# K's mixed input in halves, and written-out orders for the first two blocks' steps of an RWKV-like attention layer

## The reference

```python
xn = ln(x); sx = shift(xn) - xn
xxx = tanh((xn + sx * maa_x) @ maa_w1)            # five groups of 32 channels
x5 = xn + sx * (maa_stack + xxx @ maa_w2)         # five mixed inputs: K, W, V, R, G
w = exp(-exp(time_decay + tanh(x5.W @ decay_w1) @ decay_w2))
r, k, v = x5.R @ Wr.T, x5.K @ Wk.T, x5.V @ Wv.T;  g = silu(x5.G @ Wg.T)
for t in tokens:                                  # per head of 16 channels, s is 16 x 16
    a = k_t (outer) v_t
    out_t = r_t @ (faaaa * a + s);  s = a + w_t * s
att = groupnorm(out) * gn_w + gn_b
x = x + (att * g) @ Wo.T
xn2 = ln(x); sx2 = shift(xn2) - xn2
kk = relu((xn2 + sx2 * ffn_maa_k) @ ffn_Wk.T) ** 2
x = x + sigmoid((xn2 + sx2 * ffn_maa_r) @ ffn_Wr.T) * (kk @ ffn_Wv.T)
```

## Time and profile before

| | |
|---|---|
| median of three runs | 1561.68 us (1560.24 to 1562.09) |
| the profiled execution | 1565.06 us |
| its span, first to last instruction | 1563.2 us |
| TensorE (matmul) busy | 1509.9 us, 97% |
| VectorE, GpSimd, ScalarE busy | 909.0, 593.5, 516.0 us |
| step 0, step 1, a middle step (kt0 to kt0) | 72.00, 93.67, 93.04 us |

### The profile page before, as it was taken

The page is one execution under the profiler, slowest core; times in us unless marked ns, Lnnn a source line. Parts: engine busy times, 40 slices in busy tenths (PEclk is TensorE's granted clock), DMA queues, the critical chain, the costliest instruction groups (busy, mean ns, idle before and its releaser), DMA issues.

```text
span 1563.2 us, 50425 instructions
## 1 busy us (share of the span) xinstructions
PE 1509.9 (97%) x22156; PEld 1093.8 (70%) x22156; DVE 909.0 (58%) x1990; ACT 516.0 (33%) x910; POOL 593.5 (38%) x512
## 2 busy tenths in 40 slices
PE   8989999999999999999999999999999999999888
PEld 7867776768677676776767677676776767777564
DVE  3566666466584755667466575655667465564542
ACT  1323333324233233423324333233423333332332
POOL 3343524335261532625244261432625244262331
PEclk9999999999999999999999999999999999999899
DMA  7011102011020211102011010201102011020110
GB/s 292 25 27 48 40 5 67 25 37 52 11 70 15 61 31 34 55 4 74 17 39 52 26 54 14 66 26 35 55 5 74 17 39 53 13 61 7 47 38 27
DMA packets 56442, 68.01 MB, mean 44 GB/s; under 512 B 23264, under 2 KB 40032, under 8 KB 55200
## 3 DMA queue, kind: packets, MB, share of 16 engines
q1 hardware_dynamic: 56224, 64.79, 13.7%
HBM read 43.75 MB, written 8.39 MB: 33 GB/s over the span
## 4 chain that ended last, share of the span: by engine, by line
PE 81%; DVE 13%; POOL 3%; issue 2%; ACT 1%; DVEq 0%; ACTq 0%; POOLq 0%
PE pair L1163 30%; PE pair L1171 20%; PE at_ps L1092 4%; DVE x L718 3%; PE at_ps L1085 3%; PE pair L1179 3%; PE att_ps L1154 2%; PE pair L1252 2%; POOL x L488 2%; PE pair L1216 2%; PE pair L1254 2%; DVE cu L631 2%; PE pair L1195 2%; PE att_ps L1141 1%; PE pair L1259 1%
## 5 line engine op out<-in xcount | busy, mean ns | idle before, releaser
L1163 PE MATMUL pair<-x,wts 128*128 128x256 f32 x2016 | 459.4, 382 | 8.2 <-POOL x L488 8.1
L1163 PEld LDWEIGHTS pair<-x,wts 128*128 128x128 f32 x2016 | 374.2, 190 | 64.3 <-ACT zt L934 9.0
L488 POOL TENSOR_TENSOR x<-x,xnT 128x1024 f32<-128x1024 f32 x79 | 171.8, 2176 | 294.0 <-DVE x L718 294.0
L718 DVE SCALAR_TENSOR_TENSOR x<-pair,vecs,sx 128x256 f32<-128x256 f32 x316 | 130.5, 475 | 239.4 <-PE pair L1195 136.7
L915 ACT ACTIVATE at<-at_ps 128x512 f32<-128x512 f32 x128 | 76.0, 594 | 291.3 <-PE at_ps L1092 253.7
L1163 PE MATMUL pair<-yT,wts 128*128 128x256 f32 x512 | 119.1, 386 | 1.5 <-DVE yT L806 1.5
L1171 PE MATMUL pair<-wts,cen 128*128 128x512 f32 x240 | 112.9, 613 | 3.2 <-DVE x L718 2.5
L1092 PE MATMUL at_ps<-rm,kc 128*16 128x128 f32 (+1 forms) x2048 | 111.1, 276 | 3.2 <-issue 3.2
L1171 PE MATMUL pair<-wts,yT 128*128 128x512 f32 x240 | 110.9, 605 | 1.7 <-POOL yT L526 1.7
L1171 PE MATMUL pair<-wts,sx 128*128 128x512 f32 x240 | 109.1, 598 | 0.0
L1163 PEld LDWEIGHTS pair<-yT,wts 128*128 128x128 f32 x512 | 95.9, 192 | 16.8 <-DVE gT L750 2.9
(11 more groups left out here) (197 smaller groups left out, 2486.6 us busy)
## 6 DMA issues: line engine op xcount, KB each, us to landing
rm<-rst SPq DMA_DIRECT2D x1024, 12.0 KB, 1.8
xu<-in_x SPq DMA_DIRECT2D x16, 512.0 KB
wts<-in_wts SPq DMA_DIRECT2D x8, 1024.0 KB, 14.4
kvs<-in_s SPq DMA_DIRECT2D x32, 256.0 KB, 3.0
s<-in_s SPq DMA_DIRECT2D x32, 256.0 KB, 3.0
x<-in_x SPq DMA_DIRECT2D x15, 512.0 KB, 4.3
out<-sx SPq DMA_DIRECT2D x15, 512.0 KB, 2.9
prev<-in_prev SPq DMA_DIRECT2D x32, 4.0 KB, 3.9
```

The lines of the kernel that those rows point to most:

```text
L488: gp.tensor_tensor(t, t, xnT[:, :, :, 1:L1].rearrange("p g b t -> p (g b) t"), ALU.add).then_inc(x5_ready, 1)
L718: last = ve.scalar_tensor_tensor(seqs(mixed(name, a), g), ps[:, :, g * L:(g + 1) * L], vecs[:, vec, g:g + 1], seqs(sx, g), ALU.add, ALU.mult)
L1163: last = pe.matmul(ps[:, g // 2, TB * (g % 2):TB * (g % 2 + 1)], wts[:, m, k, g * P:(g + 1) * P], source[:, k, :], start=(k == 0), stop=(k ...
```

## The change

K's mixed input is handed over in halves. VectorE tells of the first two of its four instructions (`mixk_half`), GpSimd adds xn in two instructions of half the size, and `k.0` starts on the first half (`x5k_half`), now with k in the outer loop, and waits for the second half at k = 2. This holds for all blocks.

Steps -1, 0 and 1 get orders, and steps 0 and 1 bank tables of their own. In step -1, VectorE makes the four `bonv` products of b = 1 early (`bonv1`), and SyncE issues `S0` of block 0 behind `M0` (`S0+`). In step 0, `chain1` shrinks to `pairs1`, which comes first on VectorE; GpSimd does `rch1` first; SyncE issues `M1` before x; `c02_1` and `c1v_1` change their banks. Step 1 has a new order on TensorE, ScalarE, VectorE and GpSimd, with `v.0` and `v.1` around `c02_1`; it had the middle steps' order before.

```diff
+BANK_SECOND = {0: BANK | {"c02_1": 1, "c1v_1": 0},
+               1: {"mixW": 0, "mixV": 1, "v": 0, "c02_1": 1, "c1v_1": 1, "mixK": 1, "mixR": 0, "z": 1, "k": 1,
+                   "decay": 0, "mixG": 1, "r": 0, "yT": 1, "xT": 1, "g": 0, "wo": 1, "x2T": 1, "c02_0": 1, "kk": 0,
+                   "c1v_0": 1, "rr": 1, "h": 0}}
...
 PE_EDGE = {...
+           1: ["kt0", "V7", "mixWV", "kv0", "A0", "aT1", "V0", "A1", "V1", "v.0", "A2", "c02_1", "v.1", "c1v_1", "V2",
+               "A3", "mixKR", "V3", "z", "k.0", "k.1", "decay", "mixG", "r.0", "kt1", "r.1", "kv1", "yT", "aT0", "A4",
+               "xT", "V4", "g.0", "A5", "wo.0", "V5", "wo.1", "A6", "g.1", "V6", "x2T", "c02_0", "A7", "kk.0", "c1v_0",
+               "kk.1", "rr.0", "h", "rr.1"],
...
 ACT_EDGE = {-1: ["z", "k", "decay", "r", "v", "xT", "g", "h", "vtm0"],
+            1: ["kt0", "dec0", "E0", "att1", "E1", "E2", "vtm1", "v", "E3", "gn_square", "z", "gn_std", "k", "decay",
+                "kt1", "dec1", "r", "yT", "E4", "xT", "E5", "E6", "g", "x2T", "E7", "att0", "vtm0", "kk", "h", "rr"],
...
 DVE_EDGE = {-1: ["mixK", "mixW", "mixR", "ln1_stats", "ln1", "mixV", "chain0", "mixG", "chain0b", "chain0c", "xT", "g",
-                 "c02_0", "c1v_0"],
-            0: ["mixV", "kv0", "mixW", "chain1", "c02_1", "c1v_1", "chain1b", "chain1c", "mixK", "mixR", "kv1", "attb0",
+                 "c02_0", "bonv1", "c1v_0"],
+            0: ["pairs1", "kv0", "mixV", "mixW", "c02_1", "c1v_1", "chain1b", "chain1c", "mixK", "mixR", "kv1", "attb0",
                 "ln1_stats", "ln1", "mixG", "xT", "chain0", "chain0b", "chain0c", "g", "c02_0", "c1v_0"],
+            1: ["attb1", "kv0", "mixV", "mixW", "chain1", "c02_1", "gn_sum", "c1v_1", "mixK", "mixR", "gn_var",
+                "chain1b", "gn_rec", "chain1c", "mixG", "kv1", "attb0", "ln1_stats", "ln1", "chain0", "xT", "wo",
+                "ln2_stats", "ln2", "x2T", "g", "xr", "c02_0", "c1v_0", "chain0b", "chain0c"],
...
-             0: ["mixV", "mixW", "rch1", "c02_1", "bon1", "rch1b", "mixK", "mixR", "ln1_stats", "mixG", "rch0",
+             1: ["mixV", "mixW", "rch1", "gn_sub", "c02_1", "bon1", "mixK", "mixR", "rch1b", "gn_scale", "ln1_stats",
+                 "mixG", "yT", "rch0", "ln2_stats", "c02_0", "bon0", "rch0b"],
+             0: ["rch1", "mixV", "mixW", "c02_1", "bon1", "rch1b", "mixK", "mixR", "ln1_stats", "mixG", "rch0",
                  "rch0b", "c02_0", "bon0"],
...
-SP_LAST = {LAST: ["S0", "M1", "F1", "x2@0", "x2@1", "M2", "M3", "M4", "out", "x2", "S1", "M5", "M6", "M7"],
+SP_EDGE = {-1: ["x", "F0", "M0", "S0+"],
+           0: ["M1", "x", "F1", "M2", "M3", "out", "x2", "S1", "M4", "M5", "F0", "M6", "M7", "M0"],
+           LAST: ["S0", "M1", "F1", "x2@0", "x2@1", "M2", "M3", "M4", "out", "x2", "S1", "M5", "M6", "M7"],
...
                 elif name in MIXES:
+                    t = mixed(name, a)[:, :, :].rearrange("p g (b t) -> p (g b) t", b=NB)
+                    old = xnT[:, :, :, 1:L1].rearrange("p g b t -> p (g b) t")
+                    if name == "mixK":
+                        gp.wait_ge(mixk_half, a.count(1, 1))
+                        gp.tensor_tensor(t[:, 0:TB // 64, :], t[:, 0:TB // 64, :], old[:, 0:TB // 64, :], ALU.add)\
+                          .then_inc(x5k_half, 1)
+                        t, old = t[:, TB // 64:, :], old[:, TB // 64:, :]
                     gp.wait_ge(mix_ready, a.count(5, turn_no(name, a) + 1))
...
+                    gp.tensor_tensor(t, t, old, ALU.add).then_inc(x5_ready, 1)
...
+            def columns_k(ps, source, whole):
+
+                for k in range(G):
+                    if k == G // 2:
+                        pe.wait_ge(x5_ready, whole)
+                    for g in range(2):
+                        last = pe.matmul(ps[:, 0, TB * g:TB * (g + 1)], wts[:, WK, k, g * P:(g + 1) * P],
+                                         source[:, k, :], start=(k == 0 and g == 0), stop=(k == G - 1),
+                                         skip_group_check=True)
+                return last
```

More of the change, by code:

```diff
@@ L59 @@
     "xT": 2, "h": 2,
-    "chain1": 0, "chain1b": 0, "chain1c": 0, "chain0": 1, "chain0b": 1, "chain0c": 1, "rch1": 0, "rch1b": 0, "rch0": 1, "rch0b": 1,
+    "bonv1": 1, "pairs1": 0, "chain1": 0, "chain1b": 0, "chain1c": 0, "chain0": 1, "chain0b": 1, "chain0c": 1, "rch1": 0, "rch1b": 0, "rch0": 1, "rch0b": 1,
     "ln1_stats": 2, "ln1": 2, "ln2_stats": -1, "ln2": -1, "att1": -1, "att0": 0,
@@ L243, in build @@
         wts_in = [sem(f"wts_in{m}") for m in range(8)]
+        mixk_half, x5k_half = sem("mixk_half"), sem("x5k_half")
         s0_in, kvm_ready, decayed = sem("s0_in"), sem("kvm_ready"), sem("decayed")
@@ L292, in build @@
         for step_ in range(-2, NBLK + 2):
-            names_ = BANK
+            names_ = BANK_SECOND.get(step_, BANK)
             if step_ == -1:
@@ L370, in step @@
             def step(i, at_):
-                for name in SP_LAST.get(i, SP_ORDER if i < LAST else []):
+                for name in SP_EDGE.get(i, SP_ORDER if i < LAST else []):
                     if "@" in name:
@@ L386, in step @@
                             load_first(at_.plus(AHEAD[name]), b)
+                    elif name == "S0+":
+                        load_s0(at_.plus(1), 0)
                     elif name in ("S0", "S1"):
@@ L485, in stage @@
                 elif name in MIXES:
+                    t = mixed(name, a)[:, :, :].rearrange("p g (b t) -> p (g b) t", b=NB)
[5 more added lines that the diff above has]
+                        t, old = t[:, TB // 64:, :], old[:, TB // 64:, :]
                     gp.wait_ge(mix_ready, a.count(5, turn_no(name, a) + 1))
-                    t = mixed(name, a)[:, :, :].rearrange("p g (b t) -> p (g b) t", b=NB)
-                    gp.tensor_tensor(t, t, xnT[:, :, :, 1:L1].rearrange("p g b t -> p (g b) t"),
-                                     ALU.add).then_inc(x5_ready, 1)
+                    gp.tensor_tensor(t, t, old, ALU.add).then_inc(x5_ready, 1)
                 elif name in ("rch0", "rch1"):
@@ L584, in chain @@
                 t2p = t2[:, :].rearrange("p (f q) -> p f q", q=2)
-                if part == 0:
+                if part in ("all", "bonv"):
                     ve.wait_ge(k_ready, blk.count(1, 1))
@@ L594, in chain @@
                     last.then_inc(kchain, 1)
+                    if part == "bonv":
+                        return
+                if part in ("all", "pairs"):
                     if blk.past(2 * NBON, NBON * b):
@@ L720, in stage @@
                             vecs[:, vec, g:g + 1], seqs(sx, g), ALU.add, ALU.mult)
+                        if name == "mixK" and g == 1:
+                            last.then_inc(mixk_half, 1)
                     last.then_inc(mix_ready, 1)
                 elif name in ("chain0", "chain1"):
-                    chain(a, int(name[5]), 0)
+                    chain(a, int(name[5]), "all")
+                elif name in ("bonv1", "pairs1"):
+                    chain(a, 1, name[:-1])
                 elif name in ("chain0b", "chain1b"):
@@ L1246, in stage @@
                         pe.wait_ge(wts_in[m], 16)
-                    pe.wait_ge(x5_ready, a.count(5, turn_no(mix, a) + 1))
-                    last = columns(ps, m, mixed(mix, a), part)
+                    whole = a.count(5, turn_no(mix, a) + 1)
+                    if name == "k" and part == 0:
+                        pe.wait_ge(x5k_half, a.count(1, 1))
+                        last = columns_k(ps, mixed(mix, a), whole)
+                    else:
+                        pe.wait_ge(x5_ready, whole)
+                        last = columns(ps, m, mixed(mix, a), part)
                 elif name in ("c02_0", "c02_1"):
```

## The result

The changed kernel takes 1569.52 us in the median of six runs (1566.53 to 1571.27), the one before 1560.96 us (1559.49 to 1562.73): ratio 1.0052, 95% interval 1.0041 to 1.0064. It is slower by some 8.5 us and lies above the range of 1552 to 1566.5 us. The profiled execution took 1570.11 us, against 1565.06; that of before lies above all six of its runs (by 4.1 over their median), so the two traces differ by only 5.1.

What follows compares the result with a forecast made beforehand. TensorE is busy 1509.9 of 1563.2 us, so only its idle and slow time can be won. Halves -4.3, step 0 -6.85, step 1 +10.3 sum to -0.85: 1560.8 us, range 1558 to 1564, wider 1552 to 1566.5.

Steps and rivals of the forecast that it cites:

- the sum of step 1: Step 1's new order: +7.9 us for waits and work, +2.4 for half clock, together +10.3 us; bounds 0 to +15.
- I take two, partly idle: +2.4: TensorE in step 1: two half-clock stretches of 3.41 us, each costing 1.7 if full of work, +2.4 us together.
- Rival 2: Step 1: five half-clock stretches full of work cost 8.5 us instead of 2.4, giving 1566.8 us; chance 0.22.
- before xT: TensorE's wait in step 1 for ln1_stats, GpSimd's root and ln1 behind attb0, less aT0 and A4: 1.9 us.
- the wait before A2: TensorE in step 1 waits for the masked copies M2, queued behind M1: 0.4 us.
- the walk's 101.55: Upper figure for step 1 without half clock, by pieces added one by one; the lower was 100.9 us.
- +7.9: Step 1 before half clock: 100.9 to 101.55 us instead of 93.67, so 7.9 us longer.
- r.0 and kk.0: TensorE's waits in step 1: 1.8 us for ScalarE's table load and exponentials, 1.05 for VectorE's x2T and g.
- The objection from ScalarE's page: Step 1: a table switch costs about 2.66 us, not 1.28, so r.0 waits 3.2 us, the sum 1.4 higher.
- The halves: K's mixed input in halves: k.0 starts 0.36 us earlier in 12 undisturbed steps, -4.3 us.
- Step 0: Earlier M1, bonv1 and pairs1 bring c02_1 forward 4.9 us, no half clock saves 2.0; in sum -6.85 us.
- Rival 1: Step 1's new order works, losing its waits and half clock: 1542 us, chance 0.07; halfway 1553 to 1558, chance 0.30.

Runs made afterwards that it cites:

- e6: The changed kernel with GpSimd's mixG in step 1 waiting until VectorE has done ln1: 1563.10 us, ratio 1.0013 of the kernel before.
- e10: The changed kernel with step 1's GpSimd mixG behind VectorE's ln1 and products without use in TensorE's waits of step 1: 1561.18 us, ratio 0.9996.
- e3: The kernel before with the new orders and bank table of step 1 only: 1578.20 us, ratio 1.0106.
- e1: The kernel before with K's mixed input in halves and nothing else: 1554.92 us, ratio 0.9955.
- e2: The kernel before with the edits of steps -1 and 0 only: 1557.25 us, ratio 0.9966.
- e4: The changed kernel with step 1 put back to the middle steps' order and table: 1552.48 us, ratio 0.9938.
- e5: The changed kernel with products without use filling TensorE's idle gaps in step 1: 1566.56 us, ratio 1.0028.

## Why the prediction was wrong

**The step that failed is the sum of step 1**, +10.3 us forecast and +18.7 measured. Two of its terms were too small.

1. *"I take two, partly idle: +2.4"*, for the half clock, with stretches of 3.41 us. There were four, 23.9 us long in all, at the waits before A1, before mixG, before xT and before c02_0. They slow the work by 9.85 us and cost 5.1 us of the step in the profiled execution, shown by the products without use: 2.7 more than forecast. Rival 2 named this mechanism and "from four stretches on"; its price of 8.5 us took the slowed work as lost, and half of it covers waits.
2. *"before xT: ln1_stats (1.5), GpSimd's root (1.0), ln1 (1.0) behind attb0, less aT0 and A4: 1.9"*. It was 5.70. The prediction had read the collision of VectorE with GpSimd for the chain (1.14 us alone, 3.04 beside GpSimd) and asked about it for the chain only. It took ln1 at its undisturbed 1.0 although its own GpSimd list puts mixG and yT right behind the root that releases ln1. This cost 3.8 us of waiting; of the 5.8 us that e6 gives back, the other 1.9 belong to the clock and are part of the 5.1 above.

Together they make 6.5 of the 8.4 us missing. Another 1.0 is the wait before A2 (1.36, forecast 0.4), seen only once the clock was repaired; the last 0.9 is spread over small pieces, among them the 0.35 us before z that belong to the clock. Removing both causes (e10) takes 9.05 us off the step and leaves it 1.8 us above the walk's 101.55 without half clock; the kernel's 1561.2 us beside the forecast 1560.8 owe something to luck, as said at e10. The other 8 to 9 us of the 18.7 are the waits that the order itself places, which the prediction had.

Two slips of its sum are small. Its 16.15 and 84.75 us make 100.9, while its +7.9 goes by 101.55; and step 1 of before holds 5.5 us of idle by the earlier trace rows (93.67 less 88.15), not 5.7.

**Right in step 1:** the other waits by place, the six above 0.5 us also by cause, and in size within 0.4 us but for r.0 and kk.0. The one before mixG, for K's release by chain1c, is 2.67 of forecast 2.4. The objection from ScalarE's page does not hold here. Timeline of ScalarE:

```profile
180.04 1.02 ACT L939 ACTIVATE kT<-pair 128x1024 f32<-128x1024 f32 x1 [6.96 <-DVE k L700]
181.08 1.28 ACT L972 ACT_TABLE_LOAD   x1
182.38 1.57 ACT L972 ACTIVATE w<-pair,vecs 128x256 f32<-128x256 f32 x4
```

The table load takes 1.28 us and the exponential begins 0.02 after it: no drain is on the path (the Trainium skill, ScalarE: Activation LUTs, "What ACT_TABLE_LOAD costs", has 2.66 us for both). r.0 waited 1.01 us, less than the 1.8 by the row, since mixG at half clock covered 1.86 instead of 1.1; in e3, with mixG at full clock, it waited 1.72.

**The halves: right in mechanism, 0.42 for 0.36 us a step.** Timeline around `k.0` of a middle step, as the earlier trace rows:

```profile
468.43 1.18 POOL L511 TENSOR_TENSOR x<-x,xnT 128x512 f32<-128x512 f32 x1 [1.36 <-DVE x L747]
...
469.57 1.17 POOL L515 TENSOR_TENSOR x<-x,xnT 128x512 f32<-128x512 f32 x1
...
470.75 0.28 ACT L967 ACTIVATE zt<-pair 128x128 f32<-128x128 f32 x1
...
471.08 3.72 PE L1207 MATMUL pair<-x,wts 128*128 128x256 f32 x16 [0.16 <-ACT zt L967]
```

GpSimd's two halves take 1.18 and 1.17 us, the second ends before k = 2, and ScalarE's zt is what `k.0` waits for now, 0.16 us. e1 gives 7 us for this part alone where 4.7 were forecast: 5.0 in twelve middle steps, 0.95 in step 0, where the half clock is 3.41 us long instead of 6.83; the rest lies where "issue" stalls and the end of the program differ from one trace to the other.

**Step 0: -6.1 for -6.85.** M1, M2, pairs1 and the banks did as forecast, with no half clock. TensorE around `c02_1`:

```profile
81.25 0.23 PE L1118 MATMUL at_ps<-rm,kc 128*28 128x32 f32 x3 [1.17 <-issue]
...
82.08 1.12 PE L1301 MATMUL pair<-bonv,headall 128*128 128x512 f32 x2
...
86.04 0.57 PE L1118 MATMUL at_ps<-rm,kc 128*4 128x32 f32 x46 [0.16 <-DMA rm<-rst]
```

`c02_1` starts 8.6 us after kt0 and not 7.35, for a stall of 1.17 us named "issue" in the middle of A1; this is what the prediction left open as stalls that may fall elsewhere. A2 waits 0.16 us for M2, forecast 0.45. By e2, step 0 alone is worth 0.34%, 5 us.

**Rival 1** (the new order works: 1542 us in full, 1553 to 1558 halfway) was wrong for this order. Another order came to 1547.6, but hardly below the 1552.5 of no new order in step 1 at all (e4).

## What to carry to other kernels

When a hand-written order is walked before it is run, the walk needs two more columns beside each name's wait: which instruction of the neighbour engine that shares the port runs at that moment, and how slow the matmuls behind each wait become. An instruction that the critical path waits for should be kept clear of long GpSimd additions by one wait on the GpSimd side, which moves the collision to work with slack. An order that leaves waits of 2 to 3 us in several places pays for them twice, and products without use recover only the part of the second price that covers no other wait.

## What the runs showed of the hardware

- VectorE's two instructions of line 712, one tensor input each, took 4.86 us beside two GpSimd additions back to back and 1.00 us otherwise: they did not share the time, each ended 0.28 us behind one of GpSimd's (201.12 and 200.83, 203.59 and 203.31). GpSimd's second took 2.52 us, 2.35 in the median. In the kernel before none of the 62 instructions of this form was held; in e3 and e5 the same two were, at 4.86 and 4.9 us.
- The four falls of TensorE to 1.2 GHz in step 1 stand at waits of 2.76, 2.67, 5.70 and 2.12 us. In the other order one fall stands behind the wait of 2.52 us, and with products in that wait there is none. The waits of 1.02 and 1.13 us had none of their own. The length of a wait does not tell by itself: in e3 a fall stands at one of 1.25 us, and a wait of 2.12 us in step 2 of the changed kernel (before 257.47) had none.
- A masked copy of 12 KB costs SyncE 0.59 us to issue in the median of the changed kernel's 1024, and 1.95 at most; eight took 5.0 to 6.2 us in the rows shown.
